# A graph kernel's lists gathered straight from the edge arrays, its degrees sent in two parts, its root and its row of factors rearranged

## The reference

```python
edge_index = jnp.stack([src, dst]); batch0 = jnp.zeros((3125,), jnp.int32)
x = _layernorm(x + _L0_gnn_ref(x, W1, b1, W2, b2, edge_index))    # two graph convolutions
x = _layernorm(x + _L1_gnn_ref(x, src, dst, ...))                 # mean over neighbours, then a GRU cell
x = _layernorm(x + _L2_gnn_ref(x, edge_index, edge_attr, ...))    # sum of edge attributes, three dense layers
x = _layernorm(x + _L3_gnn_ref(x, src, dst, ...))                 # two SAGE convolutions

# what the first layer does with the degrees
deg = segment_sum(ones, col);  dis = where(deg > 0, rsqrt(max(deg, 1)), 0)
out = segment_sum((h @ W)[row] * (dis[row] * dis[col])[:, None], col) + b
```

## Time and profile before

| | us |
|---|---|
| median of 3 runs | 881.16 (880.61 to 881.54) |
| the profiled execution | 881.7 |
| its span, first to last instruction | 880.0 |
| TensorE busy | 810.2 (92%) |
| VectorE busy | 606.4 (69%) |
| ScalarE busy | 324.6 (37%) |
| GpSimd busy | 13.1 (1%) |

### The profile page before, as it was taken

One profiled execution on the slowest core, in us unless ns is written; L12 is line 12 of the kernel. 1 busy time (PEld: TensorE's weight loads), 2 busy tenths in 40 slices (PEclk: granted clock), 3 DMA queues, 4 the chain that ended last, 5 costly groups with the idle time before them and its releaser, 6 DMA issues.

```text
span 880.0 us, 16142 instructions
## 1 busy us (share of the span) xinstructions
PE 810.2 (92%) x6422; PEld 719.5 (82%) x6422; DVE 606.4 (69%) x927; ACT 324.6 (37%) x578; POOL 13.1 (1%) x35
## 2 busy tenths in 40 slices
PE   7299999999996999989989998989987999999995
PEld 5299999999986999889989997444445999699994
DVE  4499999999964776778867873657457554135654
ACT  0044544454454322332345232344334322432242
POOL 2300000000000000000000000000000000000000
PEclk9998999999996999999998999989998999999997
DMA  9845888888851000000000000000000000000001
GB/s 274 180 88 130 177 178 173 181 176 174 182 120 25 1 1 1 1 1 1 1 11 9 1 1 3 1 0 13 1 0 24 1 0 1 0 1 0 1 24 51
DMA packets 167389, 48.59 MB, mean 55 GB/s; under 512 B 155034, under 2 KB 165854, under 8 KB 167307
## 3 DMA queue, kind: packets, MB, share of 16 engines
q1 hardware_dynamic: 154176, 45.36, 22.2%
q10 hardware_dynamic: 12012, 0.83, 0.9%
q0 software_dynamic: 1120, 1.29, 0.6%
HBM read 45.44 MB, written 8.41 MB: 61 GB/s over the span
## 4 chain that ended last, share of the span: by engine, by line
PE 83%; DVE 8%; DMA 3%; issue 2%; SPq 2%; ACT 2%; DVEq 0%; ACTq 0%
PE bank L1650 19%; PE bank L1651 19%; PE bank L1586 14%; PE bank L1576 10%; DMA lists_d<-in_src 2%; PE bank L1853 2%; PE bank L1785 2%; PE bank L1861 2%; PE bank L1842 2%; PE bank L1711 1%; PE bank L1841 1%; PE bank L1904 1%; PE bank L1905 1%; PE bank L1663 1%; PE bank L1789 1%
## 5 line engine op out<-in xcount | busy, mean ns | idle before, releaser
L1650 PE MATMUL bank<-stage,f_hi 125*128 125x392 f32 x1000 | 347.6, 348 | 5.1 <-issue 2.3
L1651 PE MATMUL bank<-stage,f_lo 125*128 125x392 f32 x1000 | 341.5, 341 | 0.0
L1092 DVE CAST stage<-counts 125x2352 fp32r<-125x2352 uint8 x120 | 164.3, 1380 | 78.6 <-PE bank L1651 78.4
L1650 PEld LDWEIGHTS bank<-stage,f_hi 125*128 125x128 f32 x1000 | 189.2, 189 | 6.5 <-issue 5.7
L776 ACT ACTIVATE stage<-counts 125x1568 fp32r<-125x1568 uint8 x80 | 108.1, 1351 | 230.5 <-PE bank L1651 226.8
L1651 PEld LDWEIGHTS bank<-stage,f_lo 125*128 125x128 f32 x1000 | 189.0, 189 | 0.6
L1586 PE MATMUL bank<-tmp,wb 128*65 128x25 f32 x2000 | 133.3, 221 | 0.2 <-DVE tmp L1044 0.2
L1586 PEld LDWEIGHTS bank<-tmp,wb 128*65 128x65 f32 x2000 | 130.0, 145 | 0.7 <-DVE tmp L1044 0.5
L730 ACT ACTIVATE counts<-bank 125x500 uint8<-125x500 f32 x188 | 87.5, 537 | 44.3 <-PE bank L1576 43.5
L1576 PE MATMUL bank<-rowb,xT 128*128 128x125 bf16 x1250 | 89.0, 228 | 7.4 <-DVE rowb L1024 3.8
L1021 DVE TENSOR_TENSOR xT<-xT,tmp 128x2560 bf16<-128x2560 bf16 (+1 forms) x63 | 92.7, 1472 | 1.3 <-ACT rowb L710 1.2
(11 more groups left out here) (211 smaller groups left out, 704.5 us busy)
## 6 DMA issues: line engine op xcount, KB each, us to landing
wb<-in_edge_attr SPq DMA_DIRECT2D x125, 256.0 KB, 3.9
lists_d<-in_dst SPq DMA_DIRECT2D x1, 3104.0 KB
lists_d<-in_src SPq DMA_DIRECT2D x1, 3104.0 KB
wa<-in_x SPq DMA_DIRECT2D x12, 125.0 KB
out<-wl SPq DMA_DIRECT2D x6, 250.0 KB
xT<-in_dst SPq DMA_DIRECT2D x63, 4.0 KB, 3.5
xT<-in_dst ACTq DMA_DIRECT2D x62, 4.0 KB, 3.0
wb<-in_L_gnn_w_ih SPq DMA_DIRECT2D x1, 384.0 KB, 3.6
```

The source lines that it names most:

```text
L1092: nc.vector.tensor_copy(set_buffer(u, m), counts[:, SETS[u][0]:sum(SETS[u]), chunk(pair * 2 + off)]).then_inc(s["set_d_ready"], 1)
L1650: mm(bank[h][:, 0:CH], f_hi[:, first + k, :], rhs[:, k, :], start=(first + k == 0), stop=False)
L1651: last = mm(bank[h][:, 0:CH], f_lo[:, first + k, :], rhs[:, k, :], start=False, stop=(first + k == HI - 1))
```

## The change

Four edits, all before the first neighbour sum.

1. *Lists.* The table and its tail are gone, and so are their loads and GpSimd's wait. GpSimd gathers from `dst` and from `src` straight, 256 entries from a given edge on: two gathers for each of the five quarters, into `wa` and no longer into `f_hi`. The first edge is 33 times the count, at most E - 256. Comparisons and sums are made in two parts: columns 0 to 124 first, then 125 to 625. TensorE now multiplies a spread column of ones with the comparison, so each partition has the whole row of counts; VectorE picks its own by a product with the identity and a sum along the row. A further operation on the flag excepts lists cut at the end of the edges. The sortedness test stands between the two parts.
2. *Degrees.* The first 3000 are written once group 60 is kept and loaded back, and only the last 125 follow after counting. The load of `w_hh` stands behind the last one.
3. *Root and order.* ScalarE loads the root's table ahead (an operation on a constant) and takes the root before it copies weights' transposes and fold. TensorE makes and reads the flag before the weights' transposes and fold. ScalarE makes high halves before it copies the fold. VectorE splits biases after the low halves.
4. *Row.* The factors are split into three bf16 parts by four small operations, and `row` is 75 bf16 products with `ident_bf` in place of 25 float products.

```diff
-            for k, ids in enumerate((dst, src)):
-                for g0, g1 in ((0, BULK), (BULK, DIRECT)):
-                    sp.dma_start(lists_d[g0:g1, k * SLOTS:(k + 1) * SLOTS],
-                                 bass.AP(ids.tensor, GE * g0, ap=[[GE, g1 - g0], [1, SLOTS]])).then_inc(s["table_out"], 16)
...
+            deg_row = deg_d.rearrange("(a n) -> a n", a=1)
+            sp.wait_ge(s["ea_kept"], PAIRED // EW // 2)
+            sp.dma_start(deg_row[:, 0:PAIRED], eaT[DE:DE + 1, 0:PAIRED]).then_inc(s["deg_out"], 16)
+            sp.wait_ge(s["deg_out"], 16)
+            for r in range(2):
+                sp.dma_start(dis_col[:, r:HI - 1:2], deg_d[0:PAIRED].rearrange("(h l r) -> r l h", l=LO, r=2)[r]).then_inc(s["deg_in"], 16)
             sp.wait_ge(s["ea_kept"], NGP)
-            sp.dma_start(deg_d.rearrange("(a n) -> a n", a=1), eaT[DE:DE + 1, :]).then_inc(s["deg_out"], 16)
+            sp.dma_start(deg_row[:, PAIRED:NP], eaT[DE:DE + 1, PAIRED:NP]).then_inc(s["deg_out"], 16)
...
+            sp.wait_ge(s["deg_out"], 32)
+            sp.dma_start(dis_col[:, HI - 1:HI], deg_d[PAIRED:N].rearrange("(l a) -> l a", a=1)).then_inc(s["deg_in"], 16)
             sp.dma_start(raw[:, 8:11, :], p["L1_gnn_w_hh"].rearrange("(g p) n -> p g n", g=3)).then_inc(s["raw_in"], 16)
...
-            pool.wait_ge(s["table_out"], 6 * 16)
             for q in range(NQ):
                 pool.wait_ge(s["idx_made"], q + 1)
-                nc.gpsimd.indirect_dma_start(lists_i[:, q * 2 * SLOTS:(q + 1) * 2 * SLOTS], None, lists_d,
-                                             bass.IndirectOffsetOnAxis(list_idx[:QL, q:q + 1], 0)).then_inc(list_in[q], 16)
+                for k, ids in enumerate((dst, src)):
+                    nc.gpsimd.indirect_dma_start(lists_i[:, (2 * q + k) * SLOTS:(2 * q + k + 1) * SLOTS], None, ids.rearrange("(e a) -> e a", a=1),
+                                                 bass.IndirectOffsetOnAxis(list_idx[:QL, q:q + 1], 0)).then_inc(list_in[q], 16)
...
+            nc.scalar.activation(small[:, 0:1], mean_w[:, :], ACT.Sqrt)
+            act.wait_ge(s["in_ready"], 1)
+            nc.scalar.activation(dis_tmp[:, :], in_inv[:, :], ACT.Sqrt).then_inc(s["sqrt_made"], 1)
...
-            act.wait_ge(s["in_ready"], 1)
-            nc.scalar.activation(dis_tmp[:, :], in_inv[:, :], ACT.Sqrt).then_inc(s["sqrt_made"], 1)
...
+            def compare(q0, q1):
+                for g in range(GP):
+                    nc.vector.tensor_scalar(before[:, g, q0:q1], block_no[:, q0:q1], last_dst[:, g:g + 1], None, ALU.is_gt).then_inc(s["before_made"], 1)
+            def list_starts(q):
+                b, at_q = (0, 0) if q == 0 else (1, (q - 1) * QL)
+                nc.vector.scalar_tensor_tensor(picked[:, q * QL:(q + 1) * QL], bank[b][:QL, at_q:at_q + QL], float(GE), ident[:QL, :QL],
+                                               ALU.mult, ALU.mult, accum_out=first_edge[:, q:q + 1]).then_inc(s["dve_w"], 1)
+                dve.wait_ge(s["dve_w"], landed.next())
+                nc.vector.tensor_scalar(list_idx[:QL, q:q + 1], first_edge[:, q:q + 1], float(E - SLOTS), None, ALU.min).then_inc(s["idx_made"], 1)
...
+            compare(*INDEX_BANKS[0])
+            dve.wait_ge(s["const_made"], 7)
+            dve.wait_ge(s["before_summed"], 1)
+            list_starts(0)
+            edge_starts(0)
...
+            compare(*INDEX_BANKS[1])
             dve.wait_ge(s["slots_clean"], 1)
             make_lists(0)
+            dve.wait_ge(s["before_summed"], 2)
+            list_starts(1)
+            edge_starts(1)
...
+            for q in range(2, NQ):
+                list_starts(q)
...
+            nc.vector.tensor_copy(dis_part[:, 0, :], dis_col[:, :]).then_inc(s["dis_split"], 1)
+            dve.wait_ge(s["dis_split"], 1)
+            nc.vector.tensor_tensor(dis_rest, dis_col[:, :], dis_part[:, 0, :], ALU.subtract).then_inc(s["dis_split"], 1)
+            dve.wait_ge(s["dis_split"], 2)
+            nc.vector.tensor_copy(dis_part[:, 1, :], dis_rest).then_inc(s["dis_split"], 1)
+            dve.wait_ge(s["dis_split"], 3)
+            nc.vector.tensor_tensor(dis_part[:, 2, :], dis_rest, dis_part[:, 1, :], ALU.subtract).then_inc(s["dis_split"], 1)
...
+            for b, (q0, q1) in enumerate(INDEX_BANKS):
+                for g in range(GP):
+                    pe.wait_ge(s["before_made"], GP * b + g + 1)
+                    last = mm(bank[b][:, 0:q1 - q0], ones_bf[:LO, :].to_broadcast([LO, D]), before[:, g, q0:q1], start=g == 0, stop=g == GP - 1)
+                last.then_inc(s["before_summed"], 1)
...
+            pe.wait_ge(s["flag_part"], 2)
+            mm(bank[3][0:1, 0:1], g_any[:LO, :], mean_w[:LO, 0:1], start=True, stop=True).then_inc(s["flag_made"], 1)
+            taken = flag_of(pe)
+            general_products(pe, 0, taken, [("xt_kept", NGR)])
             pe.wait_ge(s["raw_in"], 64)
...
-                    last = mm(bnk[:, h * LO:(h + 1) * LO], col[:, h:h + 1].to_broadcast([LO, D]), ident[:LO, :LO], start=True, stop=True)
+                    for k in range(3):
+                        last = mm(bnk[:, h * LO:(h + 1) * LO], parts[:, k, h:h + 1].to_broadcast([LO, D]), ident_bf[:LO, :LO], start=(k == 0), stop=(k == 2))
```

145 lines of the change are left out of this document (62 added, 83 removed).

## The result

The changed kernel took 854.93 us in the median of four runs (853.96 to 858.32), the kernel before 880.88 (879.91 to 881.54). The ratio is 0.9713, with a 95% interval from 0.9684 to 0.9742: 26 us faster. The forecast was 859.4, its range 853 to 869. The profiled run is the slowest of the four: 858.32 us, span 856.6, against 881.7 and 880.0 before.

The account below looks back on a forecast made before the run. The chain lies on TensorE for 83% of 880.0 us, leaving it at the start and between counting and first sum. Gains of 13.0 + 9.0 - 0.2 = 21.8 us take 881.2 to 859.4; range 853 to 869.

Parts of the forecast that it names:

- First comparison: Start, VectorE: 25 comparisons of 125 columns at 0.18 us each, 4.6 us from 5.16, ending at 9.8.
- rival C: Start: the second comparison's columns run at half rate, 0.42 us each, 3.4 us more, 862.8 us in all; chance 0.13.
- Gathers: Start, GpSimd: first pair issued at 11.0, landing at 20.0, hidden; second lists wait up to 2.3 us, 0.6 taken.
- Rival E: Gathers are cut into 4-byte elements: 78 us a pair, about 1250 us in all; chance 0.03.
- Start: Up to the first counting product: 30.3 against 43.92, 13.6 us earlier, of which 13.0 were taken.
- keep step: Start: TensorE's 25 new products of 125 columns, 0.113 us each even at the slow rate, follow VectorE's comparisons.
- Counting: Early groups are bound by VectorE, 6.05 us apart at either clock; the shift survives, an extra flag operation costs 0.2.
- rival B: Second quarter's gathers land at 33, or the slow rate reaches groups 4 and 5; 864.7 us; chance 0.13.
- my own sign: Counting: the forecast is wrong if products of group 4 and later take 2.26 us for 20.
- Middle: Counting's end to first neighbour sum: degrees sooner, root ahead, TensorE late next; sum starts 9.0 us earlier, bounds 5.5 and 10.
- the root with no table load: Middle, ScalarE: the table's 1.28 us load is done while waiting; with the earlier root, factors come at 268.0 against 277.97.
- Behind: After the first sum product: work left as it is, so the shift carries through to the end one for one.

Follow-up runs that it names:

- start_only: The kernel before with the new start alone (direct gathers, first quarter ahead, no table); 868.43 us, ratio 0.9858 to the kernel before.
- middle_only: The kernel before with the new middle alone (degrees in two parts, root ahead of fold, bf16 row); 874.60 us, ratio 0.9893.
- again: The changed kernel timed and profiled once more with no edit; 857.48 us, ratio 0.9727 to the kernel before.
- not_ahead: The changed kernel with the second, longer comparison put back ahead of the first lists' starts; 861.30 us, ratio 0.9778 to the kernel before.
- flag_spread: The changed kernel with the sixth counting group's four flag operations put one each into four groups; 856.50 us, ratio 0.9722 to the kernel before.
- table_late: The changed kernel without the root's table loaded ahead on ScalarE; 855.47 us, ratio 0.9706 to the kernel before.
- root_late: The changed kernel with the root behind ScalarE's copies of the fold and no table loaded ahead; 866.83 us, ratio 0.9807 to the kernel before.
- deg_pe: The changed kernel with the last 125 degrees taken through TensorE instead of written to DRAM and loaded; 853.82 us, ratio 0.9685.
- deg_pe_spread: The changed kernel with the last 125 degrees through TensorE and the four flag operations spread over four groups; 851.84 us, ratio 0.9661.
- late_split: root_late with VectorE's four operations splitting the factors put ahead of the seven that scale the features; 865.88 us, ratio 0.9811.

## Why the prediction was right, and where it missed

*First comparison: right in kind, a little dear.* 0.167 us a step where I had 0.18, 0.273 where I had 0.286. The comparisons began at 6.81, though, and not at 5.16, since the destinations land some 2 us later in every profile with the new start. My sum took their landing over from the kernel before, and no rival had it. So the first gather was issued at 12.25 and not at 11.0. That the long comparison ends at 20.91, as forecast, is luck: 1.65 us of late begin against 0.8 saved in the comparisons (10.99 us where I had 11.8) and 0.8 between them (3.1 where I had 3.9).

*Alignment.* The 501-column operation begins at an odd 16-bit element and takes 0.273 us a step, not 0.42. So rival C is out. This row agrees with section 5.1 of the Trainium skill's page "Vector Engine (DVE) Microarchitecture Reference", by which 4-byte alignment makes no difference. The Trainium skill's page "VectorE: DVE Perf Modes", section "Mode 2×_1P — pack two bf16 into one 32-bit read", asks for that alignment; here the missing alignment cost nothing that the row shows.

*Gathers.* No wait for the first pair, 1.09 us for the second against 0.6 taken. Rival E is out, with 1.21 to 2.69 us of issue for each gather.

*Start: the size nearly right, the cause misnamed.* I wrote that the quarter ahead moves the gather and that the copy's removal brings little. The second holds (1.1 us by the rows) as long as nothing else changes. The first doesn't: of the 14.9 us the quarter ahead is 4.8, and some 10 come from the table's removal and TensorE's new products together, neither of which would have brought them alone. I had the new products in the sum, as "keep step", without saying that VectorE had idled 14.38 us for the old ones. Against 13.6 the profile shows 14.8 us to the first counting product. The term is VectorE's stretch between the long comparison and the first one-hots: 20.83 to 26.13 us is 5.3, and I had 2.8 + 3.7. In start_only 13.9 (43.92 + 215.5 less 29.06 + 216.5) were left at the end of the counting, where I had 12.8 (13.0 less 0.2 for the flag's operation).

*Counting: the rate.* One-hots of groups 1 to 4 stood 6.05 to 6.09 apart as forecast (those of groups 0 and 1 stood 7.14 apart, with the wait for the second list), and the slow rate cost nothing there. What I left out of the forecast and had, at another place, as half of rival B is a dip later on, in groups 8 to 11: it cost 3.5 us in one profile of the changed kernel and nothing in the other. By my own sign the forecast would have been wrong in the first: 20 products took 2.27 us at 66.93 and again at 72.48. The dip is no property of the new start: middle_only, with the old one, has it too (219.1 us). In the kernel before the clock was 0.50 from 70 to 73 us and no step lost more than 0.2 by it.

*Middle: right, by 0.1 to 1.5 us.* Forecast -9.0. Versions with the whole new middle (changed, again, middle_only, not_ahead, flag_spread; table_late lacks only the table's load ahead) took 18.1 to 20.4 us, that is 8.2 to 10.5 less than the 28.6 before. TensorE was late next, as said: fold, row and first sum product follow each other without a wait, and the row runs at the high level. The steps inside: the last degrees were there 4.5 us behind the memset in one profile and 5.6 in the other (forecast 5.0), the row took 4.29 and 4.58 us (forecast 5.0), and between the fold's end and the row's begin there is no idle. Its reason was partly wrong: "the root with no table load" was a gain that the load's place in the queue gives for nothing (table_late), and what carries the root's step is its place ahead of the fold. root_late, which also puts the high halves behind the fold's copies on ScalarE, lost 7.1 us; that place alone was not measured.

*Behind: not one for one.* I carried the shift to the end. The stretch behind the first sum product took 592.0 us before and 588.1 after, in code that is the same. Over all fourteen profiles it takes 588.0 to 588.9 in nine and 590.3 to 592.0 in five, and the five have no edit in common: both kinds of start, of middle and of row are among them. Still, the two with the old start have 592.0, and the changed kernel, again, not_ahead, table_late, flag_spread, deg_pe and deg_pe_spread all have 588.0 to 588.6, so an effect of the two halves together isn't excluded. The same stretch before and after, from 295 to 330 us behind the first sum product, same columns as above:

```profile
583.02:618.02 35.00, 30.36 (x96) 15.28 (x96) 20.94 (x64) 17.63 (x37) 0.00 (x0) 0.90 0.02 8
```

```profile
563.55:598.55 35.00, 30.87 (x100) 15.65 (x100) 22.57 (x66) 17.35 (x37) 0.00 (x0) 0.95 0.03 8
```

The granted clock is 0.90 in one and 0.95 in the other. In this stretch it is 0.90 in four of the five long profiles and 0.95 in the nine short ones. The fifth, start_only, has 0.95 here and loses elsewhere: in the first 10 us behind its first sum product its clock is 0.83, with 54 products, where the others have 1.00 and 62 to 65. The traces show how the clock falls behind idle time of TensorE, here ahead of the flag in the kernel before:

```profile
264.00:266.00 2.00, 0.69 (x6) 0.69 (x7) 0.00 (x0) 0.00 (x0) 0.00 (x0) 1.00 0.56 57
266.00:268.00 2.00, 0.51 (x5) 0.27 (x3) 0.00 (x0) 1.25 (x3) 0.00 (x0) 0.64 0.34 2
268.00:270.00 2.00, 0.00 (x0) 0.00 (x0) 0.39 (x3) 0.00 (x0) 0.00 (x0) 0.50 0.15 1
```

That such dips make the 4 us is argued from these windows; no run forced one.

*The sum.* Forecast -21.8. By its own steps: start and lists bring 13.9 (14.8 less 0.9) where I had 12.8 (13.0 less 0.2), 1.1 more; the middle lies between 0.8 less and 1.5 more; the stretch behind brings up to 3.9 more; dips in the counting 0 to 4.4 less. The medians say 25.4 to 26.0. That the profiled pair gives 23.4, so near to 21.8, is in part luck: 5.9 us lost in the counting, where I had allowed 0.8, stand against 3.9 gained behind it, where I had nothing, and against 1.2 and 1.5 more in start and middle. The mechanism of the middle was right, that of the start was right in its steps and misnamed in its cause. The error of 4.5 us in the time (3.6 to 4.2 in the gain) is of the size of what differs between single profiles of one kernel.

## What to carry to other kernels

Before costing a wait or a move, list what each engine on the way does meanwhile. At the start the chain of waits named only the table, while products on TensorE ended 1.3 us ahead of it; two thirds of the gain needed both gone. The root's move back cost 7 us where I had 2 to 4: seven scaling operations stood between it and its consumer (2.7 us of the middle by late_split's trace), the fold's copies began 2.4 us later than I had let them, and the row behind the wait was slow. In these traces an idle stretch of TensorE was paid twice, as idle and in the products behind it: the same 75 products took 6.48 and 6.59 us behind 8.08 and 4.26 us of idle, and 4.29 to 4.72 behind none. One profile is one sample of the clock: cut the span at fixed instructions and compare the terms over several versions before explaining a difference of 4 us.

## What the runs showed of the chip that I had not expected

- A table load of 1.28 us on ScalarE ran at 249.80, at once behind the work before it, while its own operation waited to 253.18 for VectorE.
- 125 values in one row of one partition came to 125 partitions in 0.65 us (249.39 to the reduction at 250.04) through one product with a single column and one VectorE operation; the write to DRAM and the load from it had taken 4.5 to 5.6 us from memset to reduction.
- The counting runs at 3.26 us a group with TensorE at 1.00, where VectorE sets the pace, and took 5.56 us for one with it at 0.50, where VectorE waited (69.31 to 74.87 in the changed kernel). TensorE is busy for 3.00 us of 3 in both cases, so its busy share does not tell the one from the other; the count of products in the window does, 31 against 55. The clock column does not always tell either. In the early groups of the kernel before it reads 1.00 over 59 products in 6 us, the rate that goes with 0.50 above:

```profile
56.00:62.00 6.00, 6.00 (x59) 5.93 (x58) 5.83 (x12) 2.18 (x6) 0.00 (x0) 1.00 0.42 90
```
